# One transformer layer with routed experts: third block's norm before the last division, base sums turned behind the tiles, odd final additions on TensorE

## The reference

```python
x = x + attention(layernorm(x), qkv_w, qkv_b, out_w, out_b)
xf = layernorm(x).reshape(-1, 128)
shared = (silu(xf @ shared_gate.T) * (xf @ shared_up.T)) @ shared_down.T
probs = softmax(xf @ gate_w.T)                       # 8 experts
topw, topi = top_k(probs, 2); topw = topw / (topw.sum(-1) + 1e-20)
routed = sum over e of (silu(xf @ expert_gate[e].T) * (xf @ expert_up[e].T)) @ expert_down[e].T * comb[:, e]
out = x + shared + routed                            # comb: topw scattered to topi; the hidden width is 352
```

## Time and profile before

| | us |
|---|---|
| median of three runs | 971.55 |
| lowest, highest | 968.47, 974.1 |
| the profiled execution | 968.54 |
| its span, first to last instruction | 966.7 |
| PE busy | 915.7 |
| VectorE, ScalarE, GpSimd busy | 716.6, 701.6, 725.2 |

### The profile page before, as it was taken

How to read it: one execution, slowest core, us unless ns; L and a number is a source line. 1 busy time by engine, 2 the same in 40 slices (tenths; PEclk the granted TensorE clock), 3 DMA queues, 4 the chain that set the end, 5 groups by cost and what they waited for, 6 DMA issues and landing times.

```text
span 966.7 us, 25810 instructions
## 1 busy us (share of the span) xinstructions
PE 915.7 (95%) x10271; PEld 757.0 (78%) x10271; DVE 716.6 (74%) x1755; ACT 701.6 (73%) x877; POOL 725.2 (75%) x457
## 2 busy tenths in 40 slices
PE   7889999999999999999999999999999979879991
PEld 6558888888888888888888888888888766449991
DVE  5978797879786978887787869786878355646665
ACT  3038878888888888888888888888788965235661
POOL 1228889898888888888988898888788978454441
PEclk8779999999999999999999999999999999999996
DMA  3321344544544454445440514141312305312214
GB/s 107 87 60 30 89 87 96 105 111 80 121 79 113 80 120 80 112 79 120 81 111 26 119 40 102 44 110 44 72 43 48 141 1 209 98 40 64 60 46 134
DMA packets 70228, 81.88 MB, mean 85 GB/s; under 512 B 8912, under 2 KB 54098, under 8 KB 68064
## 3 DMA queue, kind: packets, MB, share of 16 engines
q1 hardware_dynamic: 67840, 76.03, 33.2%
q0 software_dynamic: 2272, 4.22, 1.2%
HBM read 21.79 MB, written 25.20 MB: 49 GB/s over the span
## 4 chain that ended last, share of the span: by engine, by line
PE 85%; DVE 8%; ACT 2%; DMA 2%; issue 2%; SPq 0%; POOL 0%; DVEq 0%; POOLq 0%; ACTq 0%
PE bg L1203 14%; PE st L1283 13%; PE st L1284 13%; PE pv L1315 7%; PE pv L1317 7%; PE pv L1319 6%; PE bg L1193 3%; PE bg L1154 3%; PE bg L1155 2%; PE bg L1156 2%; PE bg L1213 2%; DVE row_max L981 2%; PE st L1296 2%; PE bg L1452 1%; PE bg L1443 1%
## 5 line engine op out<-in xcount | busy, mean ns | idle before, releaser
L578 POOL TENSOR_TENSOR p_lo<-prob,p_hi 128x1024 f16<-128x1024 f32 x320 | 617.2, 1947 | 135.0 <-ACT p_hi L688 133.7
L687 ACT ACTIVATE prob<-st,p_bias 128x1024 f32<-128x1024 f32 x320 | 330.0, 1031 | 119.1 <-PE st L1284 89.0
L688 ACT ACTIVATE p_hi<-st,p_bias 128x1024 f16<-128x1024 f32 x320 | 328.1, 1025 | 0.0
L981 DVE TENSOR_REDUCE row_max<-bg 128x1 f32<-128x512 f32 x384 | 255.5, 686 | 14.5 <-PE bg L1203 8.7
L1283 PE MATMUL st<-big 128*128 128x512 f32 (+3 forms) x640 | 241.9, 380 | 2.4 <-ACT p_hi L688 1.6
L1203 PE MATMUL bg<-big 128*128 128x512 f32 (+3 forms) x640 | 236.5, 399 | 4.6 <-DVE v_parts L971 2.1
L1315 PE MATMUL pv<-v_parts,p_hi 128*128 128x65 f16 x2176 | 235.1, 194 | 1.4 <-POOL p_lo L578 1.4
L1315 PEld LDWEIGHTS pv<-v_parts,p_hi 128*128 128x128 f16 x2176 | 200.1, 96 | 45.1 <-issue 32.9
L1317 PE MATMUL pv<-v_parts,p_hi 128*128 128x64 f16 x2176 | 233.9, 195 | 0.0
L1284 PE MATMUL st<-big 65*128 65x512 f32 (+3 forms) x640 | 232.5, 369 | 0.0
L1319 PE MATMUL pv<-v_parts,p_lo 128*128 128x65 f16 x2176 | 232.2, 192 | 0.0
(11 more groups left out here) (216 smaller groups left out, 1143.2 us busy)
## 6 DMA issues: line engine op xcount, KB each, us to landing
big<-big SPq DMA_DIRECT2D x192, 128.0 KB, 2.3
row_dram<-fill SPq DMA_DIRECT2D x8, 1290.0 KB, 10.8
big<-part_dram SPq DMA_DIRECT2D x8, 1088.0 KB, 8.7
big<-big SPq DMA_DIRECT2D x16, 512.0 KB, 4.3
part_dram<-stage_parts SPq DMA_DIRECT2D x32, 176.0 KB, 2.5
part_dram<-stage_parts SPq DMA_DIRECT2D x16, 192.0 KB, 3.8
stage_raw<-ffn_w SPq DMA_DIRECT2D x16, 176.0 KB, 3.0
v_parts<-row_dram SPq DMA_DIRECT2D x39, 64.5 KB, 1.8
```

The lines of the kernel that those rows point to most:

```text
L578: nc.gpsimd.tensor_tensor(o, a, b, ALU.subtract).then_inc(p_lo_ready, 1)
L687: nc.scalar.activation(o32, src, ACT.Exp, bias=p_bias[:], scale=D ** -0.5)
L688: nc.scalar.activation(o16, src, ACT.Exp, bias=p_bias[:], scale=D ** -0.5).then_inc(exp_done, 1)
L981: nc.vector.tensor_reduce(row_max[:, t, c:c + 1], bank, AX_X, ALU.max).then_inc(bg_drained, 1)
```

## The change

The last head's att_y of block 2 moves from slot 17 behind the ranks in slot 18. The norm of block 2 is done whole in slot 19. VectorE's fourth norm (last_norm) takes hidden(2) before its inverse deviation, now of one block, and hidden(3) between its two Newton steps. base_sum(2) comes before hidden(10) and late_tiles. The tasks base and ScalarE's four copies go. tile_x(0) and tile_x(1) get banks of their own and stand before down(11); base_sum(3) stands behind tile_x_lo(1). Behind the tiles PE multiplies each tile of res by the identity into PSUM (sum_bank), sixteen products, and they wait for nothing but the last tile. For the eight even token tiles VectorE adds as before, with the first addition reading PSUM. For the eight odd ones VectorE builds sixteen diagonal matrices of the weights (weight_diag), PE accumulates diagonal × y onto the sum, two products for each tile, and ScalarE copies the bank to res. SP's store of a chunk waits for both.

```diff
 LAST_HEAD: -16: [("logits", 0)], 17: [("att_y", PAIRS - 1, 2)], 18: [("ranks", 0)], 19: [("turn", 2)]}
            +16: [("logits", 0)], 18: [("ranks", 0), ("att_y", PAIRS - 1, 2)], 19: [("turn", 2)]}
 TAIL:      -..., ("ranks", 1), ("base", 0), ("base", 1), ("base", 2), ("base", 3)]
            +..., ("ranks", 1)]
+        t_x_bank = [bg[:, 0, 0:P], bg[:, 1, 0:P], pv[:, 0:P]]
+        odd_bank = [st[:, 1, 0, :], st[:, 1, 1, :], bg[:, 0, :], pv[:, :]]
+        def sum_bank(t):
+            c = t // 2
+            return odd_bank[c % 4][:, tile(c // 4)] if t % 2 else st[:, 0, c // 4, tile(c % 4)]
+        weight_diag = xn[:, :].rearrange("p (r t d) -> p r t d", r=2, d=P)
 # sync, each chunk's store
                 sp.wait_ge(out_ready, c + 1)
+                sp.wait_ge(odd_ready, c + 1)
 # scalar
             silu_of(3)
+            second_copy(2)
             silu_of(4)
             turned_xn_copy(2)
+            silu_of(5)
             turned_xn_copy(3)
-            silu_of(5)
-            second_copy(2)
             second_copy(3)
-            for q in range(6, 10): silu_of(q); then base_copy(0), silu_of(10), base_copy(1), silu_of(11), base_copy(2), base_copy(3)
+            for q in range(6, STEPS): silu_of(q)
 ...
             router_exps()
+            act.wait_ge(base_turned, 1)
+            for c in range(CHUNKS):
+                t = 2 * c + 1
+                act.wait_ge(y_summed, c + 1)
+                nc.scalar.copy(rows[:, t], sum_bank(t)).then_inc(odd_ready, 1)
 # vector, task turn of blocks 0 to 2 (was 0 and 1)
+                    statistics(b, bank)
                     att = ("att_y", PAIRS - 1, b)
                     inverse_deviation(4 * b, 4, bg[:, NUMBER[att] % BGRING]).then_inc(bg_drained, 1)
                     dve.wait_ge(bg_drained, drained(att))
                     rows_of(attn, bank, b).then_inc(bg_drained, 1)
-                    elif b == 2:
-                        nc.vector.tensor_copy(x_rows, bank).then_inc(bg_drained, 1)
-                    else:
-                        own(inverse_deviation(8, 8, None))
-                        rows_of(attn, x_rows, 2).then_inc(ln_rows, 1)
-                        rows_of(attn, bank, 3).then_inc(bg_drained, 1)
+            def last_norm():
+                bank = bg[:, NUMBER["turn", 3] % BGRING]
+                dve.wait_ge(bg_ready, drained(("turn", 3)))
+                statistics(3, bank)
+                hidden(2)
+                own(inverse_deviation(12, 4, None, lambda: hidden(3)))
+                rows_of(attn, bank, 3).then_inc(bg_drained, 1)
 ...
-            background_task(("turn", 3))
-            hidden(2)
-            hidden(3)
-            early_tiles()
+            last_norm()
             hidden(4)
             base_sum(0)
+            early_tiles()
+            hidden(5)
             table(0, EARLY)
-            hidden(5)
 ...
             hidden(9)
+            base_sum(2)
+            hidden(10)
             late_tiles()
-            hidden(10)
-            base_sum(2)
             hidden(11)
-            base_sum(3)
 ...
             tile_x_lo(1)
+            base_sum(3)
 ...
             router_weights()
+            for r in range(2):
+                nc.vector.tensor_tensor(
+                    weight_diag[:, r], ident[:].rearrange("p (o d) -> p o d", o=1).broadcast_to([P, NT // 2, P]),
+                    top_w[:, 1:NT:2, r:r + 1].broadcast_to([P, NT // 2, P]), ALU.mult).then_inc(diag_ready, 1)
+            dve.wait_ge(base_turned, 1)
             for c in range(CHUNKS):
                 dve.wait_ge(y_landed[c], 16)
-                for r in range(2):
-                    for t in range(NT)[chunk(c)]:
-                        res[t] = y_rows[t, r] * top_w[t, r] + res[t]
+                t = 2 * c
+                rows[:, t] = y_rows[:, t, 0] * top_w[:, t, 0] + sum_bank(t)   (then_inc y_added, wait for it)
+                rows[:, t] = y_rows[:, t, 1] * top_w[:, t, 1] + rows[:, t]    (then_inc out_ready)
 # tensor
             down(2)
+            background_task(("rows_t", 2))
             gate_up_shared(5)
-            background_task(("rows_t", 2))
             background_task(("rows_t", 3))
 ...
-            background_task(("base", 0)) to ("base", 3), between the last six down products
-            down(11)
             def tile_x(i):
                 pe.wait_ge(x_gathered[i % XRING], 16 * (i // XRING + 1))
-                wait(pe, t_x_lo_ready, i)
-                nc.tensor.transpose(pv[:, 0:P], gathered[i % XRING][:, 0:P], ident[:]).then_inc(t_x_ready, 1)
+                if i >= AHEAD:
+                    pe.wait_ge(shared_summed, NB)
+                    pe.wait_ge(t_x_lo_ready, i)
+                nc.tensor.transpose(t_x_bank[min(i, 2)], gathered[i % XRING][:, 0:P], ident[:]).then_inc(t_x_ready, 1)
-            for e in range(EXPERTS):
-                pe.wait_ge(e_landed[e], 16)
-            pe.wait_ge(shared_summed, NB)
             pe.wait_ge(table_ready, 1)
+            pe.wait_ge(bg_drained, BG_TOTAL)
             for i in range(AHEAD): register load, tile_x(i)
+            down(11)
+            for e in range(EXPERTS):
+                pe.wait_ge(e_landed[e], 16)
 ... # behind the tile loop
+            pe.wait_ge(t_h_done, TILES); pe.wait_ge(t_h_lo_ready, TILES); pe.wait_ge(t_x_lo_ready, TILES)
+            for t in range(NT):
+                mm = nc.tensor.matmul(sum_bank(t), res[:, tile(t)], ident[:], start=(t % 2 == 0 or t < 8),
+                                      stop=(t % 2 == 0), skip_group_check=True)
+            mm.then_inc(base_turned, 1)
+            pe.wait_ge(diag_ready, 2)
+            for c in range(CHUNKS):
+                t = 2 * c + 1
+                pe.wait_ge(y_landed[c], 16)
+                wait(pe, odd_ready, c - 3)
+                nc.tensor.matmul(sum_bank(t), weight_diag[:, 0, c], y_rows[:, t, 0, :], start=False, stop=False, ...)
+                nc.tensor.matmul(sum_bank(t), weight_diag[:, 1, c], y_rows[:, t, 1, :], start=False, stop=True, ...
+                                 ).then_inc(y_summed, 1)
```

More of the change, by code:

```diff
@@ L57 @@
              9: [("att_t", PAIRS - 1, 1), ("rows_t", 0)], 10: [("att_y", PAIRS - 1, 1)], 11: [("turn", 1)],
-             13: [("rows_t", 1)], 15: [("att_t", PAIRS - 1, 2)], 16: [("logits", 0)], 17: [("att_y", PAIRS - 1, 2)],
-             18: [("ranks", 0)], 19: [("turn", 2)]}
+             13: [("rows_t", 1)], 15: [("att_t", PAIRS - 1, 2)], 16: [("logits", 0)], 18: [("ranks", 0), ("att_y", PAIRS - 1, 2)],
+             19: [("turn", 2)]}
 STAGE_SLOTS = (9, 15)
@@ L136 @@
 TAIL = [("att_t", PAIRS - 1, 3), ("att_y", PAIRS - 1, 3), ("turn", 3), ("rows_t", 2), ("rows_t", 3), ("logits", 1),
-        ("ranks", 1), ("base", 0), ("base", 1), ("base", 2), ("base", 3)]
+        ("ranks", 1)]
 STAGED = [(e, j) for e in range(EXPERTS) for j in range(3)]
@@ L386, in rows_done @@
         def rows_done(eng, b):
[L388 to L391 removed]
+            eng.wait_ge(bg_drained, drained(("turn", b)))
         def chunk(c):
@@ L708, in _ @@
                         split_out_weights(i + 1)
-            def base_copy(b):
-                act.wait_ge(bg_drained, NUMBER["base", b])
-                act.wait_ge(bg_ready, drained(("base", b)))
-                nc.scalar.copy(res[:, blk(b)], bg[:, NUMBER["base", b] % BGRING, :]).then_inc(bg_drained, 1)
             def silu_of(q):
@@ L804, in own, with statistics, inverse_deviation @@
                 dve.wait_ge(router, steps[0])
-            def inverse_deviation(t0, n, scratch):
+            def statistics(b, bank):
+                for t in range(4):
+                    last = nc.vector.bn_stats(stats[:, 4 * b + t, :], bank[:, tile(t)])
+                last.then_inc(ln_stats, 1)
+                dve.wait_ge(ln_stats, b + 1)
+                for t in range(4 * b, 4 * b + 4):
+                    last = nc.vector.bn_aggr(mean_var[:, t, :], stats[:, t, :])
+                own(last)
+            def inverse_deviation(t0, n, scratch, between=None):
                 t = slice(t0, t0 + n)
@@ L829, in inverse_deviation @@
                         own(last)
+                        if between:
+                            between()
                     y = out
@@ L1005, in background_task @@
                     b = task[1]
-                    for t in range(4):
-                        last = nc.vector.bn_stats(stats[:, 4 * b + t, :], bank[:, tile(t)])
-                    last.then_inc(ln_stats, 1)
-                    dve.wait_ge(ln_stats, b + 1)
-                    for t in range(4 * b, 4 * b + 4):
-                        last = nc.vector.bn_aggr(mean_var[:, t, :], stats[:, t, :])
-                    own(last)
-                    if b < 2:
-                        att = ("att_y", PAIRS - 1, b)
-                        inverse_deviation(4 * b, 4, bg[:, NUMBER[att] % BGRING]).then_inc(bg_drained, 1)
-                        dve.wait_ge(bg_drained, drained(att))
-                        rows_of(attn, bank, b).then_inc(bg_drained, 1)
```

(18 more changed lines are left out.)

47 lines of the change are left out of this document (21 added, 26 removed).

## The result

The changed kernel took 956.0 us in the median of four runs (954.88 to 957.87), the kernel before 970.29 us beside it (968.47 to 974.1). The ratio is 0.985, with a 95% interval of 0.9823 to 0.9877: 14 us less. The prediction was 957.0, range 951 to 963.5, with 954.5 for the profiled execution; that one took 954.88 us, with a span of 952.9 (before 968.54 and 966.7).

The account below looks back on a forecast made before the run. PE, busy 95% of the span, bounds the kernel, so gains come only where it stands still or isn't last. 12.5 + 1.5 = 14.0 us off 968.54 gives 954.5 profiled; stated 957, range 951 to 963.5.

Parts of the forecast that it names:

- (b): Start of the tiles moves only by stalls plainly removed: gain 7.5 + 1.5 = 9 us, 962.5; chance 0.08.
- (d): Low clock stays through the first expert tiles, 2.1 us more each; ten such tiles give 978; chance 0.03.
- (a): At the end, PE's loads and products do not overlap at low clock: end costs 5 us, 964; chance 0.10.
- (e): At the end, base sums are products costing four times a transpose, additions start 7 us late: 964; chance 0.02.
- (c): At the end, VectorE alone counts, loads unmoved: +3.4 us there, 955; chance 0.08.
- Third norm: Whole norm ahead of the last division: 1.0 us of delay shrinks to 0.1 behind shared gate and up products.
- Fourth norm: Behind the fourth statistics: block 3's down product starts at 836.1 instead of 840.92, 4.8 us sooner.
- The last waits: Base turns leave, sum 2 and tile_x come earlier: 11.6 us gained by tile 0's gate/up, 12.5 at tile_x 2.
- The clock: First tile's six products at full clock, 1.0 us instead of 1.9; with the clock low the gain is 11.
- The end: Last additions split between VectorE and PE: last store at 963.0 instead of 964.5, 1.5 us; bounds -5 and +3.4.

Follow-up runs that it names:

- Down-11-first: Changed kernel with down 11 and the last base sum in front of the first two tile_x, as before: 960.56 us, ratio 0.9904.
- late-sum run: Changed kernel with the third base sum behind the late tile counts and hidden product 10, as before: 960.54 us, ratio 0.9899.
- warm PE and split table: Changed kernel plus three identity products behind the base products and the late table spread over rounds 1 to 4: ratio 0.9992; repeated on another chip 955.66 us, 0.9852.
- the extra products: Three more identity products on PE behind the sixteen base products; alone on the changed kernel: 976.54 us, ratio 1.0009.
- two queues: Changed kernel with odd chunks' final loads issued by ScalarE: 974.37 us, ratio 0.9988; with spread table and three more products too: 971.61 us, 0.9932.

## Why the prediction was right, and where its terms were off

**The place of the gain.** The prediction put 12.5 us by tile_x 2 and 1.5 us at the end. Counted from the statistics, tile_x 2 came 13.8 us sooner (863.53 before, 850.42 after) and the end gave 0.6. That the profiled execution, 954.88, lies so near the 954.5 is partly luck: the start was put 1.3 us too low, the end 0.9 us too high, and the attention of this execution ended some tenths later. Rival (b), the stalls alone, gives 7.5 us by the start of the tiles and is out by the 13.8. Rival (d), a low clock through the tiles, didn't come: where the clock fell ahead of the tiles or in the first of them, it was back at 1.00 within 4 us. Rivals (a) and (e) are out by the rows of L1494 and L1486, at 0.43 and 0.23 us a product; (c) is out because PE and ScalarE, not VectorE, came last, and the end gained 0.6 us where it had 3.4.

**Third norm: right.** The division ends 5.9 us behind the third block's statistics, where I had 6.0, and PE's transposes (now L1221) start at 814.33 right behind gate and up products. The delay of 0.1 us that I had expected is the 0.15 us by which the fourth statistics follow the third's later.

**Fourth norm: right, by 0.4 us.** Down 6 was expected 17.1 us behind the statistics and came 16.7 behind them. PE shows no gap over 0.2 us from 812.4 to 847.7, as foretold.

**The last waits: the term that was too small.** From down 6 to the end of down 10 I had 11.2 us and the trace shows 11.2. Behind it I had 2.7 us until the first expert product and there are 1.4. I had kept the 0.78 us "issue" of the earlier trace rows as the price of a register load, and 0.7 us for each tile_x. In the changed order the two tile_x follow down 10 at once and start together at 847.67, 0.38 us for both; down 11, which waits for VectorE anyway, hides the rest. Down-11-first brings those waits back as 0.39 and 0.33 us behind a wait of 1.62. In these traces the wait showed where PE stood without work ahead of the load (0.78, 0.39, 0.33 us), and not where the load stood behind products that were still running; that this is the reason is my reading, and no run tests it.

**The clock.** I took the full clock for the first tile, and it held. In the sum it was worth 0.6 us. My reason, that a gap of 2 us or so leaves the clock alone where one of 3.24 lowers it, was wrong: it fell behind 2.11 us in the late-sum run and behind 2.46 in the second execution of the kernel before, and held behind 3.24 there. The one gap that was left there was 0.41 us, and the clock stayed at 1.00 in both traces of the changed kernel.

**The end: half right, and half of the gain gone.** The base products ended 3.6 us behind the tiles and not 6.1: all sixteen ran at 1.00, 0.23 us each, and PE was at work where the earlier trace rows show an idle one. Such work doesn't always find the high clock, though: in the repeated run of warm PE and split table it fell at about 933.5, within the last tile and behind waits of 0.31 and 0.87 us, and the first five base products took 2.2 us (934.22 to 936.45). In the changed kernel's trace the shorter time gained nothing, as the first chunk lands later. The last landing came 11.45 us behind the last scatter, as predicted (11.5). The term that was too small is what stands behind it. I gave it one chunk's work, 1.1 us; since chunk 7 has landed by the time that chunk 6 is done, and PE does both at 1.2 GHz in 2.1 us (948.26 to 950.33), it is 2.1 us and 0.27 us of copy with handovers, 2.4 us: the last store is issued 13.9 us behind the last scatter instead of 13.0. The Trainium skill's rule on the clock, which the prediction cites, may be worth more than the 0.4 us that I gave it: with the warm PE the end on the third chip was 1.0 us shorter. How much of that is the clock isn't settled, as the landings came sooner too, the two other traces with the extra products have 14.5 and 14.7, and the changed kernel itself has 14.3 and 13.9.

## What to carry to other kernels

Start from the stage where the busiest engine stands still, and count the work of the engine that feeds it in the order of its queue: moving the work that PE waits for, or that stands ready, in front of the rest gained 3.5 to 3.9 us at each of three places. Behind the last landing count all that is ready with it, once at each of the two clocks. Give a stall of 2 to 3.5 us two prices, with and without the low clock, and don't read which it is from one trace. Undo also the part that took the most code: here the diagonals, their products and ScalarE's copies could go without a loss that the times show. And a result from one chip is a result of that chip: run the unaltered kernel beside a surprise before you blame an edit.

## What the runs showed of the hardware

- **The clock doesn't follow the length of a gap alone.** A gap of 3.23 us was followed by a granted clock of 1.00, one of 2.11 us by 0.50. The kernel before has the same two gaps in both its traces: behind 3.24 us the clock averaged 0.62 in one and 1.00 in the other, and behind 2.46 us it was 1.00 in the one and 0.66 in the other. In the last stage the clock fell only between 1 and 2 us after PE had begun again behind 2.96 us of waiting. The Trainium skill, "TensorE: Matmul & The Clock Gate" (Part 1), says that the point of the change differs from run to run of one kernel; these two traces of one kernel agree.
- **Float32 products of 128 columns** into 128 partitions took 0.23 us from start to start at 2.4 GHz and 0.43 us at 1.2 GHz, with a new weight for each; a float32 transpose of the same size took 0.11 us at 2.4 GHz (four in 0.44), half of that.
- **Eight loads of 256 KB**, issued about 0.5 us apart on one queue, don't land evenly. VectorE waited ahead of chunks 0, 2, 4 and 6 in one execution of the changed kernel and ahead of 0, 2, 5 and 6 in the other; in both, chunk 7 was there 0.7 us behind chunk 6 at the latest. On two queues the first chunk came 1 us later (3.75 us behind its issue), and VectorE's waits behind it were 0.25 to 0.31 us.
- **ScalarE waits without a releaser** of 3 to 11 us appeared at the silu of product 4 (L720), at the copy of block 2's turned rows (L659) and at the first silu of the tiles (L757), in all five traces on two chips and in none of the other nine, seven of which are known to come from other chips. The kernel before was 6 and 8 us slower on those chips too, but was not profiled there, nor was the unaltered changed kernel run there. What holds ScalarE at these points, and whether the gain of 14 us exists on such a chip, stays open; the kernels nearest to the changed one gained 0 to 2 us on the one and 7 us on the other.
